# Grouped attention rewritten by pairs and started inside the last head of the attention before it

## The reference, cut to what matters

```python
h = h + _L1_attn_ref(_layernorm(h), ...)      # wide attention: 8 heads of 128 features
h = h + _L1_ffn_ref(_layernorm(h), ...)       # grouped attention, chosen per sequence

def gqa(x, wq, wk, wv, wo, n_kv):             # 8 heads of 16 features, n_kv of them with own keys
    q = (x @ wq)...; k = (x @ wk)...; v = (x @ wv)...
    scores = einsum('bhqd,bhkd->bhqk', q, k) / sqrt(16)
    return (softmax(scores) @ v)... @ wo

routing_input = x.mean(axis=1)                # one row per sequence
logits = relu(routing_input @ r_w1 + r_b1) @ r_w2 + r_b2
sel = argmax(softmax(logits))                 # which of 3 sets of weights this sequence takes
out = where(sel == i, gqa(x, *params[i], nkv), out)   for i in 0, 1, 2
```

## Time and profile before

| what | us |
|---|---|
| median of 3 runs (1221.4 to 1223.19) | 1221.5 |
| the profiled execution | 1227.97 |
| its span, first to last instruction | 1226.2 |

### The profile page before, as it was taken

One profiled execution on the slowest core, in us unless ns is written; L12 is line 12 of the kernel. 1 busy time (PEld: TensorE's weight loads), 2 busy tenths in 40 slices (PEclk: granted clock), 3 DMA queues, 4 the chain that ended last, 5 costly groups with the idle time before them and its releaser, 6 DMA issues. The chain is left out here.

```text
span 1226.2 us, 20562 instructions
## 1 busy us (share of the span) xinstructions
PE 1010.3 (82%) x7048; PEld 707.9 (58%) x7048; DVE 650.5 (53%) x1865; ACT 600.3 (49%) x1338; POOL 410.8 (34%) x560
## 2 busy tenths in 40 slices
...
GB/s 90 77 114 101 143 102 85 126 88 85 110 151 107 92 85 11 1 56 15 1 1 9 19 35 35 40 1 9 9 14 15 37 1 2 1 35 121 79 89 28
DMA packets 56903, 68.05 MB, mean 56 GB/s; under 512 B 9533, under 2 KB 50393, under 8 KB 53721
## 3 DMA queue, kind: packets, MB, share of 16 engines
...
q0 software_dynamic: 512, 1.05, 0.7%
...
q10 hardware_dynamic: 504, 0.20, 0.1%
...
## 5 line engine op out<-in xcount | busy, mean ns | idle before, releaser
L2508 DVE TENSOR_REDUCE t_nmax<-banks 128x2 f32<-128x512 f32 x256 | 168.3, 686 | 91.4 <-PE banks L2327 90.0
L2443 ACT ACTIVATE t_probs<-banks 128x512 f32<-128x512 f32 x256 | 147.5, 592 | 110.5 <-PE banks L2349 109.7
L2349 PE MATMUL banks<-t_packed 120*128 120x256 bf16 x512 | 101.7, 281 | 27.0 <-DMA t_packed<-t_mT 26.3
L2327 PE MATMUL banks<-t_packed 96*128 96x256 bf16 x512 | 100.8, 280 | 19.0 <-DMA t_packed<-t_qk_pairs 16.0
L2591 POOL TENSOR_SCALAR xhat<-t_rbuf,mv,rstd 128x128 f32<-128x128 f32 x128 | 100.1, 795 | 3.4
L2349 PEld LDWEIGHTS banks<-t_packed 120*128 120x128 bf16 x512 | 42.9, 100 | 82.8 <-issue 39.2
L2327 PEld LDWEIGHTS banks<-t_packed 96*128 96x128 bf16 x512 | 46.7, 100 | 70.3 <-issue 32.0
L2362 PE MATMUL banks<-t_probs,t_v 128*32 128x256 f32 x1024 | 82.5, 395 | 0.0
L1549 ACT ACTIVATE hid<-banks,b 128x512 f32<-128x512 f32 x64 | 43.5, 687 | 68.9 <-PE banks L1454 68.3
L1873 ACT ACTIVATE l_probs<-banks,l_shift 128x256 f32<-128x256 f32 x128 | 59.5, 472 | 31.0 <-DVE l_shift L1912 28.5
L708 POOL TENSOR_TENSOR n_rstd<-n_vareps,mhalf 128x4 f32<-128x4 f32 x4 | 4.0, 1006 | 208.2 <-DVE n_nmean L691 208.1
...
## 6 DMA issues: line engine op xcount, KB each, us to landing
...
```

What stands on the lines that cost most here:

```text
L2327: ins = pe.matmul(m.mbank[:, n % 3, i * S:(i + 1) * S], m.packed[0:MROW, 0, p, h, c + qt * P:c + (qt + 1) * P], m.packed[0:MROW, 1, p, h, ...
L2349: ins = pe.matmul(scores, m.packed[0:TROW, 1, p, h, c + kt * P:c + (kt + 1) * P], m.packed[0:TROW, 0, p, h, c:c + S], start=True, stop=True)
L2443: act.activation(m.probs[:, n % 6, :], m.sbank[:, n % 2, :], ACT.Exp).then_inc(sem["probs_ready"], 1)
L2508: dve.tensor_reduce(m.nmax[:, b, u // 4, 2 * hp:2 * hp + 2], m.mbank[:, n % 3, :].rearrange("p (i k) -> p i k", i=2), AX.X, ALU.max, negat ...
```

## The change

`emit_stages`, `emit_norms` and `choose_attention` are gone. `wide_attention` runs units 0 to 56 as before; from unit 57 on every engine follows a written list, `LAST_HEAD`, in which the rest of the last head stands among the steps of the grouped attention of the four pairs. The block has no barrier inside it. The steps, with g for the pair and 0 or 1 for the sequence in it:

- nd, np, nx: statistics (DVE), inverse root and normed rows (POOL, which took only the root before). nd g waits until both sequences of pair g are added to R.
- mm, mc, r1, rr, r2, rd: mean of a sequence by four products with a column of 1/256 on PE, then the routing, for one pair at a time.
- wa, wb: the chosen weights, those of queries and keys on DVE with features ordered by position and then by head, those of values and output on POOL (5 operations of 512 elements).
- nT, nc, Aq, Ak, V, Vc: xT, queries, keys, values; values are copied by ACT.
- pq, rq, yq, zq (and pk to zk): first part by ACT, rest by DVE, second part by ACT, third by POOL. sq, lq, sk, lk: the store and three loads of each side, on SP.
- M, m, Mp, MT, mt, x: maxima; Mp (the split) is on POOL, and x is one DMA from SBUF into 24 packed rows. S, E, AV, O, T1, TR, T2, t2, C1, C1d as before; so stores the output from R per sequence.

Three packed slots serve four pairs, so that lq 3 waits until the values of pair 0 are done. PE's two banks for small products (`lin`) are taken in turn, and a step waits until the bank's previous content is read.

```diff
...
-    for n in range(len(units) + 3):
+    for n in range(WIDE_HEAD):
...
-        scores = ("SC", n) if n < len(units) else None
-        turns = ("T", n - 2) if 2 <= n < len(units) + 2 else None
+        scores = ("SC", n)
+        turns = ("T", n - 2) if n >= 2 else None
         values = ("AV", n - 3) if n >= 3 else None
...
-    return units, order, act_order
...
+    return units, order + list(LAST_HEAD["pe"]), act_order + list(LAST_HEAD["scalar"]), order + list(LAST_HEAD["vector"])
...
+            for step, g in LAST_HEAD["sync"]:
+                chosen.sync(sp, step, g)
...
-            pool.memset(m.packed[MROW:MROW + 3, 1, :, :, :], 1.0)
+            chain = Link(pool, sem["g_pool"])
+            chosen.constants(pool, chain)
+            for step, g in LAST_HEAD["gpsimd"]:
+                chosen.gpsimd(pool, chain, step, g)
...
+                    chosen.tensor(pe, *item)
...
+                    chosen.scalar(act, *item)
...
+WIDE_HEAD = 57
+LAST_HEAD = {
+    "pe": (
...
+        ("T", 58), ("AV", 57), ("SC", 60), ("T", 59), ("AV", 58), ("AV", 59), ("SC", 61), ("SC", 62), ("mm", 0),
+        ("T", 60), ("r1", 0), ("SC", 63), ("r2", 0), ("nT", 0), ("mm", 1), ("AV", 60), ("r1", 1), ("T", 61),
+        ("Aq", 0), ("r2", 1), ("nT", 1), ("Ak", 0), ("T", 62), ("AV", 61), ("Aq", 1), ("AV", 62), ("T", 63),
...
+    "gpsimd": (
+        ("np", 0), ("nx", 0), ("np", 1), ("nx", 1), ("wb", 0), ("zq", 0), ("wb", 1), ("zk", 0), ("np", 2), ("nx", 2),
+        ("np", 3), ("nx", 3), ("zq", 1), ("zk", 1), ("wb", 2), ("zq", 2), ("Mp0", 0), ("zk", 2), ("wb", 3),
+        ("Mp1", 0), ("zq", 3), ("Mp0", 1), ("zk", 3), ("Mp1", 1), ("Mp0", 2), ("Mp1", 2), ("Mp0", 3), ("Mp1", 3),),
+    "sync": (
+        ("sq", 0), ("lq", 0), ("sk", 0), ("lk", 0), ("sq", 1), ("sk", 1), ("lq", 1), ("sq", 2), ("lk", 1), ("x0", 0),
...
+}
...
+    def sync(sp, step, g):
+        if step in ("sq", "sk"):
+            k = int(step == "sk")
...
+        elif step in ("lq", "lk"):
+            k = int(step == "lk")
+            sp.wait_ge(stored[k][g % 2], 16 * (g // 2 + 1))
+            if g >= G_SLOTS:
+                sp.wait_ge(sem["g_av"], 8 * (g - G_SLOTS) + 8)
...
+        elif step in ("x0", "x1"):
+            b = int(step[1])
+            sp.wait_ge(sem["g_mrow_sb"], 2 * g + b + 1)
+            sp.dma_start(packed[MROW:TROW, 0, g % G_SLOTS, :, b * S:(b + 1) * S],
+                         mT[0:3 * H, b, :].unsqueeze(1).broadcast_to([3 * H, H, S])).then_inc(mrow[b], 16)
...
+        for i in range(G_SLOTS):
+            chain.step(pool.tensor_copy(packed[MROW:TROW, 1, i], r.heads[MROW:TROW, :].unsqueeze(2).broadcast_to([3 * H, H, PW])))
+        pool.wait_ge(sem["loaded_ahead"], 16 * len(r.loads))
...
+        elif step == "mm":
+            pe.wait_ge(sem["g_norm"], g + 1)
...
+            bank = use()
+            for b in range(2):
+                for i in range(2):
+                    ins = pe.matmul(bank[:, b:b + 1], m.X[:, 4 * g + 2 * b + i, :], r.share[:, :], start=(i == 0), stop=(i == 1))
+            filled(ins)
...
+        elif step in ("Aq", "Ak"):
+            pe.wait_ge(sem["g_xT"], g + 1)
+            pe.wait_ge(sem["g_wqk"], g + 1)
+            bank = use()
+            for b in range(2):
+                ins = pe.matmul(bank[:, b * S:(b + 1) * S], weights(g, b, 0 if step == "Aq" else 1),
+                                m.xT[:, g * PW + b * S:g * PW + (b + 1) * S], start=True, stop=True)
...
+            if b == 0 and u == 0:
+                pe.wait_ge(packed_sem[g % G_SLOTS], 16 * 6 * (g // G_SLOTS + 1))
...
+            if u == 0:
+                pe.wait_ge(mrow[b], 16 * (g + 1))
...
+        if step == "nd":
+            dve.wait_ge(sem["added"], B * (WH - 1) + 2 * g + 2)
...
+            for i in range(4):
+                ins = dve.bn_stats(stats[:, i, :], m.R[:, 4 * g + i, :])
+            chain.step(ins)
+            for i in range(4):
+                ins = dve.bn_aggr(mv[:, g % 2, i, :], stats[:, i, :])
+            ins.then_inc(sem["g_stats"], 1)
...
+        elif step == "rd":
...
+            dve.wait_ge(sem["g_logits"], g + 1)
...
+            chain.step(dve.tensor_reduce(r.top[:, 1, :], r.key[:, :, :], AX.X, ALU.max))
+            for b in range(2):
+                ins = dve.tensor_scalar(r.hot[:, g, b, :], r.key[:, b, :], r.top[:, 1, b:b + 1], None, ALU.is_equal)
+            ins.then_inc(sem["g_hot"], 1)
...
+        elif step == "wa":
+            dve.wait_ge(sem["g_hot"], g + 1)
+            for o in range(OPTIONS):
+                for b in range(2):
+                    dst, src = weights(g, b, 0, 2), r.by_feature[:, o].rearrange("p i n -> p (i n)")
+                    if o == 0:
+                        ins = dve.tensor_scalar(dst, src, r.hot[:, g, b, o:o + 1], None, ALU.mult)
+                    else:
+                        ins = dve.scalar_tensor_tensor(out=dst, in0=src, scalar=r.hot[:, g, b, o:o + 1], in1=dst, op0=ALU.mult, op1=ALU.add)
+                if o < OPTIONS - 1:
+                    chain.step(ins)
+            ins.then_inc(sem["g_wqk"], 1)
+        elif step in ("rq", "rk"):
+            k = int(step == "rk")
+            dve.wait_ge(sem["g_first"], 2 * g + k + 1)
+            if g:
+                dve.wait_ge(sem["g_split"], 2 * (g - 1) + k + 1)
+            dve.tensor_tensor(rest[:, k], lin[turn[("Ak" if k else "Aq", g)][0]], parts[:, k, g % 2, 0 if k else 2], ALU.subtract
+                              ).then_inc(sem["g_rest"], 1)
...
+    def gpsimd(pool, chain, step, g):
+        if step == "np":
+            pool.wait_ge(sem["g_stats"], g + 1)
+            chain.step(pool.tensor_scalar(vareps[:, g % 2, :], mv[:, g % 2, :, 1], EPS, None, ALU.add))
+            pool.tensor_tensor(rstd[:, g % 2, :], vareps[:, g % 2, :], m.mhalf[:, :], ALU.pow).then_inc(sem["g_root"], 1)
+        elif step == "nx":
+            pool.wait_ge(sem["g_root"], g + 1)
+            for i in range(4):
+                ins = pool.tensor_scalar(m.X[:, 4 * g + i, :], m.R[:, 4 * g + i, :], mv[:, g % 2, i, 0:1], rstd[:, g % 2, i:i + 1],
+                                         ALU.subtract, ALU.mult)
+            ins.then_inc(sem["g_norm"], 1)
+        elif step == "wb":
+            if g == 0:
+                pool.wait_ge(sem["g_const"], 1)
+            pool.wait_ge(sem["g_hot"], g + 1)
+            dst = (m.T if g < 2 else late)[:, 8 * (g % 2):8 * (g % 2) + 8, :].rearrange("p (b i) n -> p b (i n)", b=2)[:, :, 2 * D:]
+            for o in range(OPTIONS):
+                src = r.wall[:, o, 2:4].rearrange("p i n -> p (i n)").unsqueeze(1).broadcast_to([P, 2, 2 * D])
+                ins = pool.tensor_tensor(option if o else dst, src, r.hot[:, g, :, o:o + 1].broadcast_to([P, 2, 2 * D]), ALU.mult)
+                if o:
+                    chain.step(ins)
+                    ins = pool.tensor_tensor(dst, dst, option, ALU.add)
+                if o < OPTIONS - 1:
+                    chain.step(ins)
+            ins.then_inc(sem["g_wvo"], 1)
+        elif step in ("zq", "zk"):
+            k = int(step == "zk")
...
+            pool.tensor_tensor(parts[:, k, g % 2, 2 if k else 0], rest[:, k], parts[:, k, g % 2, 1], ALU.subtract).then_inc(sem["g_split"], 1)
+        elif step in ("Mp0", "Mp1"):
+            b = int(step[2])
...
+            pool.wait_ge(sem["g_max_taken"], 16 * g + 8 * b + 8)
+            ready(pool, "MT%d" % b, g - 1)
+            chain.step(pool.tensor_copy(mp[:, :, 0:H], nm))
+            chain.step(pool.tensor_tensor(nm, nm, mp[:, :, 0:H], ALU.subtract))
+            chain.step(pool.tensor_copy(mp[:, :, H:2 * H], nm))
+            pool.tensor_tensor(mp[:, :, 2 * H:3 * H], nm, mp[:, :, H:2 * H], ALU.subtract).then_inc(sem["g_mparts"], 1)
...
-        sb("g_spare", [P, 96])
-        m.packed = packed_memory(nc, stack, "g_")
-        with ExitStack() as small:
-            wide_attention(nc, m, t, sem, settle, banks, small, route.loads)
-        m.loads, m.loads_ahead = [], []
-        emit_norms(nc, m, sem, ("X",))
-        settle()
-        m.wsel = sb("wsel", [P, B, 4, D])
-        attention_memory(nc, m, banks, stack, "g_")
-        choose_attention(nc, m, route, sem, banks)
-        chosen_attention(nc, m, route, sem, out)
+        sb("g_spare", [P, 120])
+        chosen = chosen_attention(nc, m, route, sem, banks, stack, "g_", out)
+        wide_attention(nc, m, t, sem, banks, stack, route.loads, chosen)
```

More of the change, by code:

```diff
@@ L109 @@
-TURN_AT = 4
-def layer_start(ffn, steps):
-    order = [("A", 0), ("V", 0), ("A", 1), ("V", 1)]
-    order += [("M", 0, u) for u in range(8)] + [("MT", 0), ("ML", 0)]
-    order += [("M", 1, u) for u in range(8)]
-    return order + [x for b in range(steps) for x in step_items(b, ffn, True, not ffn)]
-def layer_turn():
-    return [x for b in range(TURN_AT, TURN_AT + B) for x in step_items(b, True, False, False)]
-def layer_end():
-    return [x for b in range(TURN_AT, B + 3) for x in step_items(b, True, False, True)]
@@ L1818, in _ @@
```

(10 more changed lines are left out.)

951 lines of the change are left out of this document (282 added, 669 removed), and 61 rows, old and new, of the table LAST_HEAD.

## The result

The changed kernel takes 1192.7 us (median of 4 runs, 1191.6 to 1194.3) against 1222.2 us (median of 4 runs, 1221.4 to 1223.2; the 1221.5 given above is that of the first three). It is 29.4 us faster by the medians, whose quotient is 0.976; the ratio estimated from the runs is 0.9747, 95% interval 0.9712 to 0.9783. 43.5 were forecast, with 1178.0 us as the time and 1159 to 1199 as the range. The sign and the range held; 14 to 15 us of the gain are missing.

A forecast was written before the change was run, and what follows sets the result against it. The last 161 us were taken as a chain, not an engine at its limit. First scores at 1110.5 plus 72.2 gave 1182.7 against a span of 1226.2, 43.5 us less: 1178.0 us, range 1159 to 1199.

The forecast's parts named there:

- Sum of unit 57 earlier, nd 0 at 1054.3: Start of grouped attention: AV 57 ahead of SC 60 brings unit 57's sum forward 0.9 us, to 1054.3.
- Durations of GpSimd's steps: POOL's queue before the first Mp: norm of a pair 4.6 us, wb 6.8, splits 1.156 and a little, Mp 1.1.
- From there on I count POOL: From 1055.6 to Mp of pair 0: POOL's queue gates the first scores, 45.9 us, Mp ending at 1101.5 before contention.
- some 2 us under POOL's queue: Start: mean, routing, wa, Aq, Ak and copies are done by 1078.5, against 1080 for POOL; thin cover.
- a POOL queue with gaps: Sign of a wrong forecast, before the first Mp: POOL has gaps, and PE's chain of routing and Aq gates.
- 17.6 us from sooner first scores, 26 from a shorter part behind them: Split of the gain: first scores at 1110.5 instead of 1128.1; then pairs 2 and 3 lose their packing waits.
- Contention 2 us, bounds 0 and 6: Start: DVE and POOL slow each other; 2 us added to POOL's queue, so Mp ends at 1103.5.
- From Mp to S 7 us: Pair 0, from Mp's end through MT, a copy and x to S: 7 us, bounds 3 and 10.5.
- 72.2 us from the first S: First scores to end: eight sequences 57.4, added products 3.1, clock 3, tail 8.7; against 98.1 before.
- Rival B: After the first scores: sequences keep stalls as x1 and lk queue on SP; 17.6 us less, 1203.9 us; chance 0.15.
- Rival C: Grouped attention: TensorE stays at the low clock, 14.4 us a sequence; 14.4 more, 1235.9 us; chance 0.03.
- Rival A: Start gated by packing, not POOL's queue: S at 1102, no clock loss; 55 us less, 1166.5 us; chance 0.18.

The follow-up runs named there:

- e1: Changed kernel with VectorE's wa keeping only its two products of option 0 (2 operations a pair, not 6; output not the reference's): 1182.8 us, ratio to before 0.9665.
- e9: Changed kernel with wb waiting for the end of the same pair's wa, and wb 2 and 3 moved behind Mp1 of pairs 0 and 1: 1181.9 us.
- e2: Changed kernel with GpSimd's wb keeping only its product of option 0 (1 operation a pair, not 5; output not the reference's): 1184.6 us.
- e3: Changed kernel with wb in operations of half the size, one for each sequence (10, not 5; the work is the same): 1186.7 us, ratio to before 0.9698.

## Why the prediction was right or wrong, point by point

- **Sum of unit 57 earlier, nd 0 at 1054.3: right, and better.** nd 0 starts 212.3 us behind the mark, where the forecast's statistics started at 212.8.
- **Durations of GpSimd's steps: right.** Norm of a pair 4.6 us (1084.23 to 1088.82) for 4.6; wb 6.1 for 6.8; a split 1.15 for 1.2; Mp 1.1 for 1.1.
- **"From there on I count POOL": the step that failed.** The durations were right, but the queue had gaps of 2.3, 4.9, 4.0 and 7.7 us, the first of them for the routing of pair 0. The prediction had laid the chain of mean, routing, wa and Aq "some 2 us under POOL's queue" and called that cover thin. It counted that chain with 2 to 3 us for each wa; each took 6.2 to 7.5. Once that was so, the chain was the gate, and the "wrong" case of the last part ("a POOL queue with gaps") came about. Mp of pair 0 ended at 1112.8 - 835.4 = 277.4 us behind the mark for 262.0. The collision is about half of that: with one option in wa (e1) Mp ended at 268.8, in e9 at 269.5, and in e2, with a fifth of wb's operations, at 267.7. So some 6 to 8 us are no collision of wa with wb, and GpSimd's queue would not have been the gate without the collision either.
- **17.6 us from sooner first scores, 26 from a shorter part behind them: the first did not come.** Measured were 1.1 us later and 29.7 us shorter. From nd 0 to the first S the changed kernel takes 75.5 us, the kernel before 61.7 from its first statistics: the start gained from beginning 12.5 us sooner (212.3 for 224.8 behind the mark) and lost it again.
- **Contention 2 us, bounds 0 and 6: mis-sized, and on the wrong engine.** The rows for it were there: two operations of L2021 at 2.66 for 0.88, a factor of 3. I let it lengthen GpSimd's queue. It lengthens VectorE's: 4.4 us for each wa against the 2.4 it takes alone, and 12.6 us (e9) to 14 us (e1, e2) on the whole. The Trainium skill (SBUF — State Buffer, Who interferes with whom) says that the blocked engine waits for the other's whole instruction. e3 agrees: with GpSimd's instructions halved, wa fell from 6.8 to 4.6 us. I had multiplied that rule out (23 us) with GpSimd as the one held up, and set it aside.
- **From Mp to S 7 us: too short by 3.** S came 10.3 us behind Mp's end (1112.8 to 1123.2), since TensorE stood at Aq 3 behind wa 3. In e1 it was 5.4 (1111.0 to 1116.45), with the x rows' transfer as the last wait, and in e9 6.3 (1112.8 to 1119.05): without the stand at Aq 3 the term was 1 to 2 us too long.
- **72.2 us from the first S: right, 3.8 too much.** From the first S to the last copy of values 61.3 us for 63.5 (57.4 + 3.1 + 3), and a tail of 7.2 for 8.7. Rival B (stalls at x1, lk) did not come: the longest wait of TensorE there, until the tail, is the 0.35 us of the timeline above. Rival C did not come: 1.00 from 1128 on.
- **Rival A** (the packing and not GpSimd gates, 1166.5 us) was right in that GpSimd is no gate, but packing is none either: the first M waited for no transfer. It was wrong in the time, because it had wa at the same price.
- **The runs without the collision end near the forecast, and that is partly luck**: 341.2 us behind the mark were forecast, and 342.2 (e1), 341.8 (e2) and 343.6 (e9, complete kernel) measured. In e1 Mp ended 6.8 us late; the way to the first S took 1.6 less than forecast, and the part behind it 4.3 less. In e9 the first scores came at 275.8 for 269.0, and the part behind them gave 4 back.

What stays open: whether the low clock carries a part of what is left. The mean clock from nd 0 to the first S was 0.64 in the changed kernel, 0.70 in e1, 0.76 in e2 and 0.72 in e9. It is higher where the stretch is shorter, and no run changed it alone. Open too is what made Mp late by the 6 to 8 us that stay without the collision.
